# Local attention: tiles of 8 x 14 queries with 490 keys on average, and four images in one pipeline

## What is computed

```python
x_flat = gn(x) as [4, 3136 pixels, 96]                       # 32 groups of 3 channels
x_n = x_flat / max(norm(x_flat), 1e-12)
sims = x_n[p] . x_n[q] for the q in the 15 x 15 window of p    # -1e9 outside the image
top_sim, top_idx = jax.lax.top_k(sims, 8)
wts = softmax(top_sim)
agg = sum(wts * x_flat[top_idx])
enhanced = agg + layernorm(x_flat) * ln_w + ln_b
out = enhanced + w2 @ relu(w1 @ enhanced + b1) + b2
x = x + out
```

## Time and profile before

| | |
|---|---|
| median of 3 runs | 18239.54 us (18234.71 to 18244.22) |
| profiled execution, its own time | 18239.56 us |
| its span | 18237.8 us |
| mean granted TensorE clock | 0.911 |
| busy share of the span | PE 78%, DVE 88%, ACT 65%, POOL 67% |

### The profile page before, as it was taken

The page is one execution under the profiler, slowest core; times in us unless marked ns, Lnnn a source line. Parts: engine busy times, 40 slices in busy tenths (PEclk is TensorE's granted clock), DMA queues, the critical chain, the costliest instruction groups (busy, mean ns, idle before and its releaser), DMA issues. The chain is left out here.

```text
span 18237.8 us, 184822 instructions
## 1 busy us (share of the span) xinstructions
PE 14267.7 (78%) x39472; PEld 5890.3 (32%) x39472; DVE 16001.4 (88%) x21043; ACT 11856.0 (65%) x23997; POOL 12262.8 (67%) x5733
## 2 busy tenths in 40 slices
PE   7898878888888768888888866677777766777776
PEld 2222233333333323333333333423333332333333
DVE  6666489999999979999999987789999968999996
ACT  3555557667777646667676733368888826888882
POOL 0000079999999849999999920069988916998881
PEclk9999899999999989999999987888888888888888
DMA  1000023333333323333333310022222212222221
GB/s 27 12 18 13 21 88 107 107 107 107 107 107 107 92 87 106 108 106 107 107 106 107 106 48 16 17 67 82 80 80 79 80 31 69 81 81 80 79 80 29
DMA packets 508593, 1386.72 MB, mean 76 GB/s; under 512 B 109117, under 2 KB 157357, under 8 KB 504093
## 3 DMA queue, kind: packets, MB, share of 16 engines
q1 hardware_dynamic: 507464, 1374.90, 25.9%
HBM read 1301.95 MB, written 58.10 MB: 75 GB/s over the span
## 5 line engine op out<-in xcount | busy, mean ns | idle before, releaser
L995 PE MATMUL PS<-Hc,ident 128*128 128x448 f32 x16128 | 7474.3, 597 | 1974.8 <-POOL Hc L1307 1621.7
L1299 POOL TENSOR_TENSOR Tr<-du,BC 128x1344 f32<-128x1344 f32 x2688 | 8161.9, 3037 | 60.8 <-DVE du L1178 60.6
L995 PEld LDWEIGHTS PS<-Hc,ident 128*128 128x128 f32 x16128 | 3094.2, 204 | 6225.0 <-POOL Hc L1307 2604.8
L1117 ACT ACTIVATE PS<-dl,A 128x448 f32<-128x448 f32 x5376 | 3402.9, 633 | 2053.2 <-DVE Hr L1225 1251.8
L1307 POOL TENSOR_TENSOR Hc<-Hr,BC 128x448 f32<-128x448 f32 (+1 forms) x2688 | 3893.7, 1449 | 1027.4 <-DVE Hr L1225 940.9
L1225 DVE TENSOR_TENSOR_SCAN PS<-PS,st,Tr 128x448 f32<-128x448 f32 x3072 | 3361.0, 1137 | 143.5 <-ACT st L1131 142.1
L718 POOL MEMSET pad<- 128x348 f32 x6 | 2.3, 388 | 4044.0 <-POOLq L67 4044.0
L1232 DVE TENSOR_TENSOR Hc<-PS,BC 128x448 f32<-128x448 f32 x4480 | 2571.9, 607 | 0.0
L1125 ACT ACTIVATE PS<-cs,lneps,A 128x448 f32<-128x448 f32 x2688 | 1940.9, 722 | 173.9 <-DVE PS L1225 171.0
L1208 DVE SCALAR_TENSOR_TENSOR PS<-PS,Tr 128x448 f32<-128x448 f32 x2688 | 1655.7, 616 | 217.9 <-ACT PS L1125 207.4
L1117 ACT ACTIVATE Ar<-dl,A 128x448 f32<-128x448 f32 x2688 | 1765.4, 657 | 0.0
(11 more groups left out here) (240 smaller groups left out, 16538.4 us busy)
## 6 DMA issues: line engine op xcount, KB each, us to landing
BC<-bcscratch SPq DMA_DIRECT2D x5376, 224.0 KB, 3.6
zscratch<-zst SPq DMA_DIRECT2D x84, 224.0 KB, 2.0
bcscratch<-rows SPq DMA_DIRECT2D x336, 56.0 KB, 2.9
z<-zscratch SPq DMA_DIRECT2D x28, 672.0 KB, 4.5
xg<-mid SPq DMA_DIRECT2D x12, 1176.0 KB, 8.1
mid<-yo SPq DMA_DIRECT2D x56, 168.0 KB, 2.0
xr<-mid SPq DMA_DIRECT2D x8, 1176.0 KB, 9.3
Q<-part SPq DMA_DIRECT2D x72, 98.0 KB, 4.3
```

The source lines that it names most:

```text
L995: e.matmul(PS[:, YB + c, 0:T], K["ident"][:], Hc[:, g % NHC, c, :], start=False, stop=(nn == 15)).then_inc(y_done, 1)
L1117: e.activation(decay_at(u), dl[:, q % 2, c, :], ACT.Exp, scale=A[:, q // NT, c, nn:nn + 1]).then_inc(a_done, 1)
L1299: e.tensor_tensor(Tr[:, g % NTR], du[:, q % 2], b, ALU.mult).then_inc(t_done, 1)
```

## The change

`local_image` goes; `local` is one stage over all four images. A tile is now 8 rows by 14 columns of queries (28 per image, 112 in all). Its keys are the rectangle that its windows cover: at most 22 rows, and 21 or 28 columns (the outer and the inner two of the four tile columns), 15 rows in the first and the last band of tiles. That is 315 to 616 keys, 490 on average. Keys are cut into blocks of up to four rows (`key_blocks`): 6 blocks in a middle band, 5 in the first, 4 in the last.

`FE` is built by DMA from 28 transposes per image, in the block layout of each tile column. GpSimd copies a tile's queries side by side (`qt`) and makes the two products of the normalization. Length and variance come as two rows out of two small products per piece (`centre`, `stat`), go to DRAM, are read back folded over 112 partitions, rooted and inverted there at once, and are spread over the channels again by DMA (`row`, `fold`, `unfold`, `spread`). All small products share PSUM bank 7 and are placed at fixed steps of the image before. The weights are no longer scaled on VectorE: the sum of the 8 largest exponentials comes from ScalarE (`exponent`), which makes a diagonal matrix `dg` of its reciprocal, and `turn` multiplies by it. `similar`, `turn` and `gather` have one PSUM buffer each. The MLP of a band of four tiles follows some steps behind. The residual is added on GpSimd.

```diff
@@ the waits and products of TensorE (pe)
+            def similar(n):
+                b, i, j = tile(n)
+                ys, xs = keys(i, j)
+                nr, w = ys.stop - ys.start, xs.stop - xs.start
+                x = grid(xn[:, b % 2, :])
+                e.wait_ge(q_ready, n + 1)
+                if n:
+                    e.wait_ge(masked, n)
+                q = qt[:, n % 4, :]
+                if nr * w <= 512:
+                    a = e.matmul(PS[0:112, 0, 0:nr * w], q, x[:, ys, xs], start=True, stop=True)
+                else:
+                    for h in range(2):
+                        a = e.matmul(PS[0:112, h, 0:11 * w], q, x[:, ys.start + 11 * h:ys.start + 11 * h + 11, xs],
+                                     start=True, stop=True)
+                a.then_inc(sim, 1)
...
+            def turn(n):
+                b, i, j = tile(n)
+                e.wait_ge(chosen, n + 1)
+                e.wait_ge(diag, n + 1)
+                if n == 0:
+                    e.wait_ge(zeroed, 1)
+                else:
+                    e.wait_ge(w_kept, n)
+                for h, blocks in enumerate(key_blocks(i, j)):
+                    for k, (_, off, kn) in enumerate(blocks):
+                        a = e.matmul(PS[0:kn, 2 + h, 112 * k:112 * k + 112], E[:, n % 2, off:off + kn], dg[:, n % 2, :],
+                                     start=True, stop=True)
+                a.then_inc(w_turned, 1)
...
+            def gather(n):
+                b, i, j = tile(n)
+                if i == 0 and j == 0:
+                    e.wait_ge(fe_ld, 320 * (b + 1))
+                e.wait_ge(w_kept, n + 1)
+                if n:
+                    e.wait_ge(added, n)
+                first, rest = key_blocks(i, j)
+                blocks = [(k, q, kn) for k, (q, _, kn) in enumerate(first)] + \
+                         [(4 + k, q, kn) for k, (q, _, kn) in enumerate(rest)]
+                for u, (k, q, kn) in enumerate(blocks):
+                    a = e.matmul(PS[0:C, 4, 0:112], FE[0:kn, b % 2, j, q, :], WT[0:kn, n % 2, k, :],
+                                 start=(u == 0), stop=(u == len(blocks) - 1))
+                a.then_inc(gathered, 1)
+
+            def hidden(g, h):
+                b, i = divmod(g, 7)
+                if h == 0:
+                    e.wait_ge(added, 4 * g + 4)
+                    if g:
+                        e.wait_ge(biased, g)
+                elif g:
+                    e.wait_ge(hid_ready, 2 * g)
+                e.matmul(PS[0:C, 5 + h, 0:T], w1[:, C * h:C * h + C], xl[:, b % 2, T * i:T * i + T],
+                         start=True, stop=True).then_inc(hid_mm, 1)
...
+            for r in range(STEPS + 12):
+                b, s = divmod(r, NTL)
+                items = small_products(s) if b + 1 < NI else (None,) * 3
+                if r < STEPS:
+                    similar(r)
+                if items[0]:
+                    before(b + 1, items[0])
+                if 0 <= r - 2 < STEPS:
+                    turn(r - 2)
+                if items[1]:
+                    before(b + 1, items[1])
+                if 0 <= r - 3 < STEPS:
+                    gather(r - 3)
+                if items[2]:
+                    before(b + 1, items[2])
+                if band_step(r, 6) is not None:
+                    hidden(band_step(r, 6), 0)
+                if band_step(r, 7) is not None:
+                    hidden(band_step(r, 7), 1)
+                if band_step(r, 8) is not None:
+                    output(band_step(r, 8))
@@ VectorE (dve)
+            def mask_(n):
+                b, i, j = tile(n)
+                ys, xs = keys(i, j)
+                nr, w, s = ys.stop - ys.start, xs.stop - xs.start, n % 2
+                y0, x0 = ys.start - QR * i + 7, xs.start - QC * j + 7
+                e.wait_ge(sim, n + 1)
+                if n >= 2:
+                    e.wait_ge(expd, n - 1)
+                    e.wait_ge(replaced, n - 1)
+                if nr * w <= 512:
+                    e.tensor_tensor(S[:, s, 0:nr * w].rearrange("p (y x) -> p y x", x=w),
+                                    PS[0:112, 0, 0:nr * w].rearrange("p (y x) -> p y x", x=w),
+                                    mask[:, y0:y0 + nr, x0:x0 + w], ALU.add).then_inc(masked, 1)
+                else:
+                    e.tensor_tensor(S[:, s].rearrange("p (h k) -> p h k", h=2), PS[0:112, 0:2, 0:308],
+                                    mask[:].rearrange("p (h y) x -> p h (y x)", h=2), ALU.add).then_inc(masked, 1)
...
+            def add(n):
+                b, i, j = tile(n)
+                x = grid(xl[:, b % 2, :])[:, QR * i:QR * i + QR, QC * j:QC * j + QC]
+                if i == 0 and j == 0:
+                    e.wait_ge(xl_ready, NT * (b + 1))
+                e.wait_ge(gathered, n + 1)
+                e.scalar_tensor_tensor(out=x, in0=PS[0:C, 4, 0:112].rearrange("p (y x) -> p y x", x=QC), scalar=lb[:],
+                                       in1=x, op0=ALU.add, op1=ALU.add).then_inc(added, 1)
...
+            for r in range(STEPS + 13):
+                b, s = divmod(r, NTL)
+                more = b + 1 < NI
+                if r < STEPS:
+                    mask_(r)
+                if 0 <= r - 1 < STEPS:
+                    divide(r - 1)
+                if r < STEPS:
+                    top(r)
+                if more and s == 4:
+                    mean(b + 1)
+                if 0 <= r - 1 < STEPS:
+                    choose(r - 1)
+                if r < STEPS:
+                    negate(r)
+                if 0 <= r - 4 < STEPS:
+                    add(r - 4)
+                if more and s == 3:
+                    total(b + 1)
+                if more and s == 6:
+                    normal(b + 1)
+                if more and s == 18:
+                    inverted(b + 1)
+                if band_step(r, 9) is not None:
+                    bias(band_step(r, 9))
@@ GpSimd (pool)
+            def scale(b, u):
+                c = NT * b + u
+                cols = slice(u * T, u * T + T)
+                e.wait_ge(rl_ld[c % 2], 32 * (c // 2 + 1))
+                e.tensor_tensor(xn[:, b % 2, cols], xg[:, cols], rl[:, 1, c % 2, :], ALU.mult).then_inc(xn_ready, 1)
+                e.tensor_tensor(xl[:, b % 2, cols], xl[:, b % 2, cols], rl[:, 0, c % 2, :], ALU.mult).then_inc(xl_ready, 1)
...
+            def query(n):
+                b, i, j = tile(n)
+                if i == 0 and j == 0:
+                    e.wait_ge(xn_ready, NT * (b + 1))
+                if n >= 4:
+                    e.wait_ge(sim, n - 3)
+                e.tensor_copy(qt[:, n % 4, :].rearrange("p (y x) -> p y x", x=QC),
+                              grid(xn[:, b % 2, :])[:, QR * i:QR * i + QR, QC * j:QC * j + QC]).then_inc(q_ready, 1)
@@ removed from VectorE
-            def scale(t):
-                s = t % 2
-                e.wait_ge(divided, t + 1)
-                e.tensor_scalar(flat(E, s), flat(E, s), den[:, s, 1:2], None, ALU.mult).then_inc(scaled, 1)
```

More of the change, by code:

```diff
@@ L1773, in ssm, with tile, window, key_blocks @@
             (tail3 if lay.ratio else tail1)(chip, K, D, pair, src, dst, yacc, zd)
-def local(chip, K, D, src, dst):
+QR, QC = 8, 14
+NTL = 28
+STEPS = NI * NTL
+def tile(n):
+    b, t = divmod(n, NTL)
+    return b, t // 4, t % 4
+def window(i, j):
+    r0, r1 = max(QR * i - 7, 0), min(QR * i + 14, 55)
+    c0, c1 = max(QC * j - 7, 0), min(QC * j + 20, 55)
+    return r0, r1 - r0 + 1, c0, c1 - c0 + 1
+def key_blocks(i, j):
+    r0, nr, _, w = window(i, j)
+    if i == 0:
+        full = [(q, w * (4 * q - 3), 4 * w) for q in (1, 2, 3)]
+        return full, [(4, w * 13, 2 * w), (0, 0, w)]
+    rows = [(k, min(4, nr - 4 * k)) for k in range((nr + 3) // 4)]
+    out = [(2 * i - 1 + k, 4 * k * w, m * w) for k, m in rows]
+    return out[:4], out[4:]
+def band_step(r, lag):
+    g, rest = divmod(r - 3 - lag, 4)
+    return g if rest == 0 and 0 <= g < 7 * NI else None
+CENTRE, STAT, TURN = 9, 10, 9
+def small_products(s):
+    a = {4: ("mean", 0), 5: ("var", 0)}.get(s)
+    if CENTRE <= s < CENTRE + NT:
+        a = ("centre", s - CENTRE)
+    b = ("stat", s - STAT) if STAT <= s < STAT + NT else None
+    c = ("turn", s - TURN) if TURN <= s < TURN + 6 else None
+    return a, b, c
+def local(chip, K, D, src, dst, scr):
+    PS = chip.PS
+    order = {}
+    for b in range(NI):
+        for s in range(NTL):
+            for what in small_products(s):
+                if what:
+                    order[b, what] = len(order)
     with ExitStack() as ctx:
@@ L1779, in local @@
         W = dict(w1=sb("w1", [C, 192]), b1=sb("b1", [C, 2]), w2=sb("w2", [C, 2, C]), b2=sb("b2", [C, 1]),
[L1780 to L1806, removed]
+                 l2lg=sb("lg", [C, 1]), l2lb=sb("lb", [C, 1]), mask=sb("mask", [112, 22, 28]),
@@ L1811, in local_image @@
[L1811 to L1815, removed]
+        w_ld, xg_ld, zeroed = sems("w_ld"), sems("xg_ld"), sems("zeroed")
```

(19 more changed lines are left out.)

531 lines of the change are left out of this document (311 added, 220 removed).

## The result

| | before | after |
|---|---|---|
| median | 18238.76 us (18234.71 to 18244.22) | 18081.90 us (18073.46 to 18096.35) |
| profiled execution, its own time | 18239.56 us | 18087.81 us |
| stage, first load to the next stage's first load | 1120.3 us | 961.5 us |
| mean granted clock, from the first to the last mask addition | | 0.756 |

The ratio is 0.9915, 95% interval 0.9897 to 0.9932: 157 us faster, where I forecast 294. The direction was right, the size about half of what I said, and the time 12 us above the top of my range.

A forecast was written before the change was run, and what follows sets the result against it. VectorE's passes were taken to bound the tiles before, the gather-add loop after. Ramp 108.5, tiles 702 (668 plus 34 for the clock), drain 13 and 2.5 gave 826 us against 1120.3, hence 17945 us; range 17860 to 18070.

The forecast's parts named there:

- VectorE's step: Tiles: mask, max, replacement, `choose` and small instructions take 12.1 us per middle band, 79 us per image against 141.
- GpSimd's hold: Tiles: GpSimd products delay VectorE passes beside them; 6 us per image taken, bounds nothing and 24 us.
- signs of being wrong: Wrong if TensorE's gather wait on the addition is absent, the clock is below 0.75, or `choose` has two durations.
- "slower" rival: GpSimd holds any VectorE pass it meets, 1.95 us each, 382 us in all: time 18327 us; chance 0.03.
- The closed loop: Tiles: similar, VectorE's step, gather, MLP product and 0.3 us handovers run in series; middle band 24.5 us, image 161 us.
- The clock: Tiles: TensorE idles 1.9 to 2.6 us in steps outside normalization; mean granted clock 0.9 costs 34 us.
- The ramp: Stage start to first mask: nothing hides the first image's load and normalization; first tile at 108 us.
- The drain: Stage end: last three gathers 4 us, two MLP rounds, bias and store 9 us, then 2.5 us as before.
- my 668 at full clock: Tiles of four images: 172 us for each of three, 161 for the last, 677, less 9 counted in the drain.
- more hold-ups: Tiles: clock near 0.7 (+130 us), GpSimd's holds at upper bound (+54), slower window reads; 18060 to 18200 us; chance 0.17.
- The rival that the loop isn't paid: Tiles: additions come in time, TensorE sets the pace at 117 us per image; stage 585 us, time 17705; chance 0.08.

The follow-up runs named there:

- early add: Kernel after the change, with VectorE's add of a tile moved from the end of its step to its start, ahead of the mask: 17779.51 us, ratio 0.9758.
- two dead products: Kernel after the change, plus two unread 448-column products before the gather's wait, in steps holding nothing of the next image: 17948.34 us, ratio 0.9849.

## Why the prediction was half right

**VectorE's step: right, and GpSimd's hold: real, but hardly met.** 0.62 and 0.78 us were forecast for `choose`, and in the tiles it takes 0.622 and 0.781 on average. That says little of GpSimd, for of the 112 `choose` only three begin while a product of GpSimd runs; they are held by 0.65 us in all, where I had taken 6 us per image. The longest, on 315 keys, takes 0.95 us instead of 0.47; that `choose` has two durations was one of my signs of being wrong. In the kernel with the early add the same instructions meet more often, 15 of 112, and lose 7.2 us in all. The one held longest there:

```profile
11085.48 1.13 POOL L2228 TENSOR_TENSOR xn<-xg,rl 96x448 f32<-96x448 f32 x1
11085.51 1.59 DVE L2162 SCALAR_TENSOR_TENSOR E<-R,E 112x462 f32<-112x462 f32 x1
...
11086.57 1.53 POOL L2229 TENSOR_TENSOR xl<-xl,rl 96x448 f32<-96x448 f32 x1
...
11087.16 0.78 DVE L2171 MATCH_REPLACE8 R<-m,S 112x616 f32<-112x616 f32 x1
```

`choose`, the pass with two SBUF inputs, starts behind the first product and takes 1.59 us instead of 0.62. The second product starts while `choose` still runs and takes 1.53 instead of 1.13. The replacement, which has one SBUF input, runs beside it in its usual 0.78. So the one that starts second is held for what is left of the other, and only where VectorE reads two SBUF tiles. The Trainium skill's sentence on this (GPSIMD Engine Reference, the table of the engine, "SBUF interfaces") is borne out. It costs little in the kernel after because the instructions rarely meet there, for which I had given no row. My "slower" rival priced any pass at 1.95 us, by a row of another instruction; here the passes with one SBUF input aren't held.

**The closed loop: right, and a little short.** The wait is where I said. In the seven steps at full clock that have nothing of the next image in them it is 1.5 to 2.2 us (2.15 in the step shown; I had 1.9 to 2.6), and 2.3 at most anywhere. I had put a middle band at 24 to 27 us; the three whose clock was 1.00, which also carry products of the next image, take 27.7, and others up to 37.8. The step shown is 6.95 us; by my terms it is 3.19 + 1.15 + 0.75 + 1.03 + 0.3 = 6.42. The gather is the main part: from its start to the MLP product behind it 1.46 us pass instead of 1.15. I took its records at 0.096 us each, from 16 in 1.70 us, and for full blocks that holds: eight of the nine gaps between its ten full records are 0.096, the first is 0.145. What I had no row for is the small block that each tile of a middle band ends with, of 56 keys where the others have 112 (42 where they have 84). From 10845 to 11670, over both levels of the clock (count, busy us, mean ns):

```profile
L1944 PE MATMUL PS<-WT,FE 112*96 112x112 f32 x496 | 70.8, 296 | 58.6 <-DVE xl L2179 58.4
...
L1944 PE MATMUL PS<-WT,FE 56*96 56x112 f32 x96 | 24.4, 341 | 0.0
```

Busy time by count is 0.14 us for each record of a full block and 0.25 for each of a small one. In the step shown the two small records start 0.19 and 0.17 us behind the ones before them, and what follows starts 0.19 behind the last. The small block of `turn` does the same (0.19, 0.13). A block with half the keys costs more than a full one. Of the rest of the 0.53 us, 0.08 is the MLP product, 0.06 VectorE's step, 0.04 each `similar` and the handovers. Over the 29 steps whose clock was 1.00 I find 6.57 us on average against 6.10 by my terms, and 0.47 x 111 is 52 us.

**The clock: the step that failed.** I wrote "I take a mean of 0.9: 34 us". The clock was 0.76, and the loss at least the 109 us by which two dead products shorten the tiles (832 to 723). It failed in two ways. First, I had the row that shows a 2.53 us idle followed by half the rate and averaged it with the row at 1.00, in which the idle is 1.03 us. But the two kinds of step don't alternate. The short waits stand together where the next image's products fill them, and there the clock is full; the others have the longer wait one after the other, in the last image throughout, and they resemble the first row, not a mean of both. From the third image:

```profile
11312.00:11359.00 47.00, 44.05 (x249) 26.63 (x248) 22.22 (x58) 28.21 (x69) 3.69 (x8) 1.00 0.04 12
11367.00:11414.00 47.00, 37.61 (x171) 24.68 (x169) 19.60 (x51) 17.73 (x43) 13.50 (x16) 0.78 0.40 99
```

The waits in the two stretches:

```profile
PE PS L1944 <- DVE xl L2179: 1.7, 4, 0.8
...
PE PS L1944 <- DVE xl L2179: 8.5, 5, 2.3
```

In the first stretch, seven steps with the next image's products, the gather waits for the addition 1.7 us in all, and the clock is 1.00. In the second, six steps without them, it waits 8.5 us, and the clock is 0.78. The other two images that carry products of a next one show the same (1.00, then 0.77 and 0.66).

The other way in which it failed: I argued that a stretch at half rate leaves TensorE busier and so cures itself. It does, and that is the trouble: at the lower level the wait before the gather shrinks (0.27 us in the second step shown, 0.6 on average over the 20 steps wholly at that level), the clock comes back, the wait comes back, and the clock falls again. The level alternates all through the tiles. The Trainium skill describes this (TensorE: Matmul & The Clock Gate, "A second HAM failure mode: psum-queue depth-cycling"): short idles between groups of matmuls make the clock switch back and forth. The trace agrees, with waits of 1.5 to 2.3 us at full clock and steps at 0.50 and 1.00 by turns, and the kernel with the early add shows the cause removed.

**Hold-ups at the start.** The ramp took 101.3 us (I had 108.5). Then the first gather waits for `FE`, and the sum of the second image for its load, which stands on the queue behind the 20 transfers, a thing that I had not counted. From the timeline of the kernel after:

```profile
10831.50 0.45 SPq L2263 DMA_DIRECT2D xg<-mid  x1
...
10835.15 2.66 PE L1944 MATMUL PS<-WT,FE 84*96 84x112 f32 x10 [4.13 <-DMA FE<-FR]
...
10839.90 3.42 DVE L2104 TENSOR_REDUCE small<-xg 96x1 f32<-96x3136 f32 x1 [9.00 <-DMA xg<-mid]
```

VectorE issues in order, so the sum's 9.00 us delay the next mask too; some 10 us in all, my estimate from these waits.

**The drain** took 28.2 us from the last mask to the next stage, where I had 15.5: its MLP products run at the lower level for part of it, 3.30 us for a round as in the step above. With the early add it is 22.8 us (from 11372.9 to 11395.7), so more than half of the miss of 12.7 us is not the clock. Two MLP rounds follow the last gather, as I had them. The last gather ends 14.0 us after the last mask here and 8.6 with the early add, where I had 4; what follows takes 14.2 us in both, where I had 11.5. So I had priced the last three steps as gathers alone, without the passes of VectorE and the end of an MLP round that stand between them.

**The sum:** 826 forecast. Ramp 7 less, drain 13 more, tiles 130 more: 962. The tiles are 164 us above my 668 at full clock: some 52 are the step's size, some 10 the start, less the 17 of GpSimd's holds that I had counted and that didn't come, and what remains, 119, is the clock, for which I had 34. The dead products bear this out: they take back 109 of it and leave a clock of 0.94. The same clock priced as I did it, on 304 us of work, is 98 us. My range had its upper end, 18060, at clock 0.75. That the time lies above it at 0.76 is due to the step's size and the drain, 65 us together; the clock alone would have left it inside the range. The rival "more hold-ups", with a chance of 0.17 and 18060 to 18200 us, holds the measured time; it had named the clock near 0.7 and 130 us for it, and came about in its clock part, without its GpSimd part. The rival that the loop isn't paid was wrong for this order and is what one moved instruction makes of it: I had 17705 for it, and 17780 was measured. Of the 75 us, 60 are TensorE's work, 119 us per image where I had 104: in the last image `turn` takes 36.0 and the gather 38.3 us where I had 29.9 each, for the small blocks, while `similar` (23.6) and the MLP (21.0) are as I had them.

## What to carry to other kernels

When a change takes a buffer from an instruction that used to reach two steps back, walk the loop that it closes, and look at once for the place in the in-order queue where the release could stand earlier: here `add` at the head of the step shortened the stage by 281 us, 1.8 times what the whole change brought. When the loop leaves the matrix engine idle in every step, price its clock by the row with the nearest idle, not by a mean over the kernel. To tell the clock from the wait, put dead matmuls into the wait, and as a control into the same place where there is no wait: what comes back in the first was the clock. When a tile is cut into blocks, look at what the last, smaller block costs before you count it as a part of a full one.

## What was not expected of the hardware

- One dead product of 448 columns per step (1.0 us where about 2 were idle) shortens the stage by 105 us, two by 112.
- Records of 112 columns follow one another at 0.096 us in full blocks, before and after (112 or 84 rows or columns of weights). Records of a block of 63 keys or fewer start 0.11 to 0.19 us behind the one before, and what follows them 0.19 us, although they do less work. Which of rows, columns or the change between sizes makes the difference stays open; no run was made for it.
- A `choose` that starts while a product of GpSimd runs is held for all that is left of it but 0.12 us (in four traces, 1.10 us left: 0.97 us longer; 0.84: 0.72; 0.21: 0.08). The passes with one SBUF input aren't held.
- The transfers that build `FE` and those that spread the lengths slow each other: issued together they make the first tile 6 us later.
